# Last row blocks in float32 column groups, with w2's load and split moved, in a mixture-of-experts kernel on one core

## What is computed

```python
# x: (8, 256, 256) float32; x_rot = quaternion rotation of x times a spectral gate
logits = jnp.einsum('bsd,de->bse', x_rot, router_w) + router_b
top1 = jnp.argmax(softmax(logits), axis=-1)          # 8 experts
for i in range(8):
    h = jnp.einsum('bsd,df->bsf', x_rot, w1[i]) + b1[i]      # 256 -> 2 * 1024
    a, g = jnp.split(h, 2, axis=-1)
    y = jnp.einsum('bsh,hd->bsd', a * sigmoid(g), w2[i]) + b2[i]
    out = out + jnp.where((top1 == i)[..., None], y, 0.0)
return x + out
```

## Time and profile before

| | us |
|---|---|
| median of three runs | 216.72 |
| lowest, highest | 215.16, 495.23 |
| profiled execution | 216.05 |
| its span | 214.3 |
| granted TensorE clock, mean | 0.988 |

### The profile page before, as it was taken

How to read it: one execution, slowest core, us unless ns; L and a number is a source line. 1 busy time by engine, 2 the same in 40 slices (tenths; PEclk the granted TensorE clock), 3 DMA queues, 4 the chain that set the end, 5 groups by cost and what they waited for, 6 DMA issues and landing times.

```text
span 214.3 us, 4364 instructions
## 1 busy us (share of the span) xinstructions
PE 202.4 (94%) x1511; PEld 189.9 (89%) x1512; DVE 158.0 (74%) x308; ACT 122.2 (57%) x206; POOL 128.8 (60%) x163
## 2 busy tenths in 40 slices
PE   7999658999999999999999999999999999999992
PEld 3768524999999999999998999899999999999991
DVE  4839980589836997498889869994898469874960
ACT  2535841484918574567684868473939185745620
POOL 6004287775601878378778878887487818720752
PEclk9999997999999999999999999999999999999998
DMA  5994734979865174947499459827845691720011
GB/s 149 387 363 181 259 118 98 294 233 321 261 183 231 49 256 89 330 144 260 79 333 291 145 176 334 258 79 213 326 119 179 185 322 56 253 46 0 25 40 37
DMA packets 17540, 41.26 MB, mean 193 GB/s; under 512 B 2920, under 2 KB 11241, under 8 KB 15338
## 3 DMA queue, kind: packets, MB, share of 16 engines
q1 hardware_dynamic: 12784, 30.48, 40.0%
q0 software_dynamic: 4512, 10.50, 19.2%
q10 hardware_dynamic: 218, 0.01, 0.1%
HBM read 36.78 MB, written 6.03 MB: 200 GB/s over the span
## 4 chain that ended last, share of the span: by engine, by line
PE 65%; DVE 15%; issue 7%; POOL 6%; DMA 4%; ACT 3%; DVEq 0%; ACTq 0%
PE y_ps L1116 8%; PE y_ps L1117 8%; PE y_ps L1118 8%; PE g_ps L1096 6%; PE g_ps L1101 6%; PE g_ps L1097 5%; PE a_ps L1101 5%; PE a_ps L1097 5%; PE a_ps L1096 5%; DMA xg<-x_rows,g_idx 4%; PE y_ps L928 3%; DVE arena L821 3%; POOL out_dram L438 2%; POOL y_out L429 2%; DVE u_lo L827 2%
## 5 line engine op out<-in xcount | busy, mean ns | idle before, releaser
L438 POOL DMA_INDIRECT out_dram<-y_out,s_idx x30 | 44.0, 1465 | 42.5 <-DVE y_out L850 31.7
L573 ACT ACTIVATE arena<-g_ps,b_t 128x384 f32<-128x384 f32 (+1 forms) x64 | 34.5, 538 | 47.1 <-PE g_ps L1101 47.0
L821 DVE SCALAR_TENSOR_TENSOR arena<-a_ps,b_t,arena 128x384 f32<-128x384 f32 (+1 forms) x64 | 36.1, 563 | 31.2 <-PE a_ps L1101 28.4
L1116 PE MATMUL y_ps<-w_hi,u_hi 128*128 128x256 f32 x168 | 48.5, 289 | 0.1
L1117 PE MATMUL y_ps<-w_lo,u_hi 128*128 128x256 f32 x168 | 47.5, 283 | 0.0
L1118 PE MATMUL y_ps<-w_hi,u_lo 128*128 128x256 f32 x168 | 47.5, 283 | 0.0
L429 POOL DMA_INDIRECT y_out<-in_x_dram,g_idx x32 | 40.9, 1279 | 9.8 <-issue 9.8
L417 POOL DMA_INDIRECT xg<-x_rows,g_idx x32 | 36.5, 1141 | 14.9 <-issue 9.1
L579 ACT ACTIVATE u_hi<-arena 128x384 fp32r<-128x384 f32 (+1 forms) x64 | 30.7, 479 | 15.5 <-DVE arena L821 15.4
L712 DVE TENSOR_TENSOR w_lo<-w_raw,w_hi 128x1024 fp32r<-128x1024 f32 x32 | 37.2, 1221 | 1.8 <-ACT w_hi L526 1.4
L1096 PE MATMUL g_ps<-xr_hi,w_hi 128*128 128x256 f32 (+3 forms) x128 | 37.0, 302 | 0.6 <-ACT xr_hi L561 0.6
(11 more groups left out here) (167 smaller groups left out, 295.6 us busy)
## 6 DMA issues: line engine op xcount, KB each, us to landing
w_raw<-in_L_ffn_w_dram SPq DMA_DIRECT2D x16, 1024.0 KB, 8.2
w_raw<-in_L_ffn_w_dram SPq DMA_DIRECT2D x16, 512.0 KB, 5.0
arena<-in_x_dram SPq DMA_DIRECT2D x4, 512.0 KB, 5.9
x_rows<-arena SPq DMA_DIRECT2D x8, 256.0 KB, 3.0
b_all<-in_L_ffn_b_dram SPq DMA_DIRECT2D x1, 1024.0 KB, 5.1
xg<-x_rows,g_idx POOLq DMA_INDIRECT x32, 6.4
y_out<-in_x_dram,g_idx POOLq DMA_INDIRECT x32, 4.4
out_dram<-y_out,s_idx POOLq DMA_INDIRECT x30, 3.7
```

What stands on the lines that cost most here:

```text
L438: nc.gpsimd.indirect_dma_start(out=out_flat, out_offset=bass.IndirectOffsetOnAxis(ap=s_idx[:, i * NSUB + s:i * NSUB + s + 1], axis=0), in_ ...
L821: V.scalar_tensor_tensor(u32[:, c % (8 - SIG_RING), 0:n], pair[c % RING][0][:, 0:n], b1_t[:, bass.ds(e * (2 * NC) + c, 1)], sig[:, c % SIG ...
L1116: T.matmul(dst, u_hi[:, uv], w2_hi[:, wv], start=first, stop=False)
```

## The change

1. The size classes become 192, 256, 288, 320, 352, 512 (384 goes, 192 comes; class 192 uses the same first product as 256). Where the last block holds up to 32 or 64 tokens (classes 288, 320, 192), it is not computed from the split operands but by `part_block`: eight float32 matmuls, one per chunk, with 32 or 64 stationary columns of u32 and 256 moving columns of w2_raw. They go in turn to 4 or 2 groups of the array's columns, each group sums its own chunks in its own partitions of y_ps[1], and DVE adds the groups (`add_parts`: three adds of 32 rows or one of 64, each waiting for the one before).
2. u32 is kept whole (8 chunks, in the space of x_t) and w2_raw is kept until the second product ends. SP's load of w2 waits for mm2_done, and w1's load of the item after it comes behind w2's.
3. w2_hi_part goes from behind chunk 2 to behind chunk 4 on ACT, w2_lo_part from behind chunk 4 to behind chunk 5 on DVE.
4. Block 0 is computed ahead of blocks 2 and 1, and the part block stands in the place of the last one. The last item's adds and scatters follow this order.
5. ACT and DVE have five bodies per item (256, 288, 320, 384, 512 columns) for three.

```diff
-    SIZES = (256, 288, 320, 352, 384, 512)
+    SIZES = (192, 256, 288, 320, 352, 512)
+    PARTS = {size: (size // P, size % P) for size in SIZES if size % P in (32, 64)}
...
-            def load_tile(i, e):
+            def load_w1_again(i, e):
                 for u in range(W1U):
                     sp.wait_ge(w1_split[u], i)
                 for k in range(KH):
                     load_w1(e, k)
+            def load_w2_again(i, e):
+                sp.wait_ge(w2_split, i)
+                sp.wait_ge(mm2_done, i)
                 for h in range(W2U):
-                    sp.wait_ge(w2_split, i)
                     load_w2(e, h)
...
+            load_w1_again(1, 1)
             for e in range(1, NE):
-                load_tile(e, e)
+                load_w2_again(e, e)
+                if e + 1 < NE:
+                    load_w1_again(e + 1, e + 1)
...
+            def add_parts(i, word, sizes_here):
+                def of_sizes(left):
+                    if not left:
+                        dve.sem_inc(dve_chain, more)
+                        return
+                    s, wide = PARTS[left[0]]
+                    with dve.If(f_size(word) == SIZES.index(left[0])):
+                        rows = y_out[i % YB][0:wide, s * DIM:(s + 1) * DIM]
+                        for g in range(1, P // wide):
+                            link(V.tensor_tensor(rows, y_ps[1][g * wide:(g + 1) * wide, PLACE[s] * DIM:(PLACE[s] + 1) * DIM],
+                                                 rows, ALU.add))
...
+                    with dve.Else():
+                        count[0] = start
+                        of_sizes(left[1:])
...
+            def part_block(size, at1, at2, done=None):
+                s, wide = PARTS[size]
+                groups = P // wide
+                for c in range(NC):
+                    pe.wait_ge(pair_free[c], at2 if c >= CARRIED else at1)
+                    g = c % groups
+                    last = T.matmul(y_ps[1][g * wide:(g + 1) * wide, PLACE[s] * DIM:(PLACE[s] + 1) * DIM],
+                                    u32[:, c, s * P:s * P + wide], w2_raw[:, c * DIM:(c + 1) * DIM],
+                                    start=c < groups, stop=c >= NC - groups)
...
-                with pe.If(f_size(word) >= BLOCKS.index(3)):
+                row_blocks((0,), at1, done=outer_done)
+                with pe.If(f_size(word) >= SIZES.index(352)):
                     row_blocks((2,), at1)
-                row_blocks((1,), at1, done=outer_done)
-                row_blocks((0,), at1, done=mm2_done)
+                with pe.Else():
+                    with pe.If(f_size(word) == SIZES.index(320)):
+                        part_block(320, at1, at2)
+                    with pe.If(f_size(word) == SIZES.index(288)):
+                        part_block(288, at1, at2)
+                with pe.If(f_size(word) == SIZES.index(192)):
+                    part_block(192, at1, at2, done=mm2_done)
+                with pe.Else():
+                    row_blocks((1,), at1, done=mm2_done)
```

More of the change, by code:

```diff
@@ L49, in adaln_moe_ffn_kernel @@
     YB = 3
-    LANDINGS = (0, 1, 2, 3, 5)
+    LANDINGS = (1, 2, 3, 4)
     CONSTS = 9
@@ L280, in if_blocks, with if_width, word_registers @@
                     body(4)
+        def if_width(eng, word, body, low=0):
+            widths = (2 * P, 288, 320, 3 * P, ITEM)
+            firsts = (0, SIZES.index(288), SIZES.index(320), SIZES.index(352), SIZES.index(ITEM))
+            if low == len(widths) - 1:
+                body(widths[low])
+                return
+            with eng.If(f_size(word) < firsts[low + 1]):
+                body(widths[low])
+            with eng.Else():
+                if_width(eng, word, body, low + 1)
+        def word_registers(eng):
+            return [eng.alloc_register(f"word_at{a}") for a in range(2)]
         def word_register(eng, name):
@@ L846, in add_rows @@
+            def add_rows(i, word):
                 dve.wait_ge(mm2_done, i + 1)
                 dve.wait_ge(b2_added, i + 1)
-                for h in range(2):
-                    half = bank_rows(i, h)
-                    V.tensor_tensor(half, y_ps[h][:, :].rearrange("p (s d) -> p s d", s=2), half, ALU.add)\
-                        .then_inc(y_done[h], 1)
-            def add_last(i, blocks):
+                half = bank_rows(i, 0)
+                V.tensor_tensor(half, y_ps[0][:, :].rearrange("p (s d) -> p s d", s=2), half, ALU.add)\
+                    .then_inc(y_done[0], 1)
+                half = bank_rows(i, 1)
+                link(V.tensor_tensor(half, y_ps[1][:, :].rearrange("p (s d) -> p s d", s=2), half, ALU.add))
+                if word is not None:
+                    add_parts(i, word, list(PARTS))
+                dve.sem_inc(y_done[1], 1)
@@ L855, in add_last @@
+            def add_last(i, blocks, n, word):
                 dve.wait_ge(b2_added, i + 1)
                 dve.wait_ge(outer_done, i + 1)
-                rows = bank_rows(i, 1)[:, 0:min(blocks - 1, 2)]
-                V.tensor_tensor(rows, y_ps[1][:, :].rearrange("p (s d) -> p s d", s=2)[:, 0:min(blocks - 1, 2)], rows,
-                                ALU.add).then_inc(last_added, 1)
-                dve.wait_ge(mm2_done, i + 1)
                 for a in range(2 if blocks == NSUB else 1):
@@ L863, in add_last @@
                     V.tensor_tensor(rows, y_ps[0][:, a * DIM:(a + 1) * DIM], rows, ALU.add).then_inc(last_added, 1)
+                dve.wait_ge(mm2_done, i + 1)
+                rows = bank_rows(i, 1)[:, 0:min(blocks - 1, 2)]
+                link(V.tensor_tensor(rows, y_ps[1][:, :].rearrange("p (s d) -> p s d", s=2)[:, 0:min(blocks - 1, 2)], rows,
+                                     ALU.add))
+                add_parts(i, word, [size for size in PARTS if max(size, 2 * P) == n])
+                dve.sem_inc(last_added, 1)
                 dve.wait_ge(last_added, 3 if blocks == NSUB else 2)
```

77 lines of the change are left out of this document (48 added, 29 removed).

## The result

The changed kernel takes **238.19 us** (median of four runs, 236.15 to 241.6) where the kernel before took 215.94 on the same chip (median of four, lowest 214.4): ratio 1.1035, 95% interval 1.0972 to 1.1097. The run of 241.6 us and one of the kernel before, 495.23 us, fell in a slower state of the chip and are not in the ratio. I had forecast 218.2 with a range up to 221.5. The change makes the kernel slower by 22 us, and nothing in my range covers it.

What follows compares the result with a forecast made beforehand. PE, at 94% of the span, was taken as the bound; savings of PE work and added waits, summed by item, came to +2.0 us, giving 218.2 us, own range 216.0 to 220.6, stated range 213.0 to 221.5.

Steps and rivals of the forecast that it cites:

- The groups: PE's part blocks: about 1.0 us with groups of 32, 1.85 with 64, against 2.88 for a row block.
- The drain of the array: Rival on PE: each change of tiling mode drains the array, 1.6 us in all, 219.8 us; chance 0.05.
- The chain to w2's split: DVE and ACT work from the adds to w2_lo's end, making PE wait 0 to 1.65 us ahead of second products.
- extras: Work added behind DVE's adds: 0.43 us for three compares and a waited-for add, plus the groups' adds at 0.46 each.
- 6.07 for the chain: From gated(3) on DVE until w2 is split, with 256 columns: 6.07 us.
- The last u_lo: DVE's last u_lo before PE's second product comes later: 1.0 us more in items 1 and 6.
- a sign of being wrong: Item 4's gather on POOL: PE no longer waiting for it would show the forecast wrong; no size given.
- Bounds 0.1 and 0.9: Range in us for the three compares and waited-for add behind DVE's adds, put at 0.43.
- my rivals: Saving arrives, 211.0 us (0.20); w2 late, 221 to 224 (0.12); array drains, 219.8 (0.05); serial groups, 221 to 222 (0.03).
- w1's load at nothing: On SP, w1's load behind w2's is hidden by the first product, 11.5 us long at least, so costs nothing.
- w2 lands late: Rival: w2's DMA landing delays w2_hi and the second product in seven items, +3 to +5 us, 221 to 224; chance 0.12.
- The end of the kernel: Behind the last bank's add, DVE's part add, two compares and two linked waits: 0.8 us, all on the path.

Runs made afterwards that it cites:

- b_w2_late_2: Kernel before with only w2's load behind the second product and its split moved later: ratio 1.041; same edit as b_w2_late on another chip: 1.0183.
- after_kept_busy: Changed kernel plus one unused float32 matmul of 128 x 512 ahead of PE's wait for w2's split in each item: ratio 1.1052 to the kernel before.
- a_no_part_adds: Changed kernel without the compares and groups' adds on DVE in items 0 to 6: ratio 1.0168 to the kernel before.
- b_w2_split_moved: Kernel before with only w2's split moved later on ACT and DVE, the loads left where they were: ratio 1.0155.

## Why the prediction was wrong

**The groups (right).** 1.07 us for 1.0 and 1.95 for 1.85, both with the last matmul's tail. The drain of the array is hardly to be seen: a part block starts 0.20 to 0.32 us behind the start of the matmul before it, at full clock, where 0.12 is the pace. That is at most 0.2 us more, and PE's compares stand in the same place, so it may be either.

**The chain to w2's split (right in kind, too small).** The waits ahead of the second products, by item 1 to 7:

| | 1 | 2 | 3 | 4 | 5 | 6 | 7 | sum |
|---|---|---|---|---|---|---|---|---|
| forecast | 0 | 0.85 | 0.5 | 0.2 | 1.65 | 0.95 | 1.5 | 5.65 |
| measured | 0.88 | 1.50 | 1.44 | 1.17 | 1.47 | 1.49 | 2.32 | 10.27 |

The terms that were too small are "extras" of 0.43 (1.02 measured in item 7, 2.22 - 1.20), 6.07 for the chain (6.22 there, 6.34 in b_w2_late_2) and the hand-over from DVE to PE, which stood nowhere (0.30 there). A reader who measures a chain must measure to the waiting engine's start, not to the end of the last operation.

**The last u_lo (right).** The second products of items 1 and 6 take 9.51 us instead of 8.71, 0.80 more where I had 1.0.

**By item.** From one first product's start to the next, in us (item 7 to the end of the last matmul; "end" is from there to the end of the span):

| | 0 | 1 | 2 | 3 | 4 | 5 | 6 | 7 | end |
|---|---|---|---|---|---|---|---|---|---|
| before | 23.79 | 24.60 | 18.19 | 18.81 | 22.81 | 22.74 | 24.52 | 17.50 | 4.1 |
| changed | 23.78 | 26.44 | 23.36 | 21.22 | 22.41 | 26.30 | 27.06 | 20.38 | 7.3 |

I had forecast +0.5 for items 2 and 3 together, and they lose 7.6; for item 5 I had -0.3, and it loses 3.6. Item 0 gains nothing, though its part block saves 0.9 us: small pauses ahead of its last two chunks, its part block and item 1 take that back. And no turn waits for a gather any more, which I had named as a sign of being wrong: items 2 and 3 are late by DVE's chain now, and not by POOL.

**"Bounds 0.1 and 0.9" for the compares, and no term for the five bodies (the step that failed).** I took an item change's 0.24 us on ACT as the price of a branch and compare. That row is of a change with no packet of the instruction queue in its idle time. The five bodies are item 5 of the change, and the sum has no term for them; nor has it one for the compares' bodies that are stored and not run. Measured, the changes to items 1, 3, 4, 5 and 6 have idle time of 2.1 to 5.5 us on ACT or DVE. Five versions alone cost 8.6 us in the kernel before; the compares, run and stored, 8.2 in the changed one. None of my rivals was this.

**"w1's load at nothing".** The load did hide. w1's split did not, because DVE came to it late: 0.45 + 1.74 us.

**The turns.** Gate 5 frees the banks that the turns need. With w2_hi ahead of gate 5, the turn waits in items 2 and 5 (1.82, 0.63). I had looked only at what the second product waits for.

**The clock.** Not in the sum: about 5 us in the trace. In after_kept_busy, where a stretch moves to item 6, nothing of it is gained.

**w2 lands late (a rival).** It happened once:

```profile
96.36 1.92 ACT L562 ACTIVATE w_hi<-w_raw 128x2048 fp32r<-128x2048 f32 x1 [1.25 <-DMA w_raw<-in_L_ffn_w_dram]
```

in item 2, where w2 landed 9.2 us behind its issue; the median is 4.9. There it is not nothing: from gate 3 to the end of w2_lo it takes 7.57 us (94.18 to 101.75) for item 7's 6.22, and item 2 loses most. The same wait, 1.2 to 2.5 us, stands in item 2 in every trace of the changed kernel's variants with one buffer but a_no_part_adds, which has it in item 4 (2.2 us). In the kernel before, b_w2_late against b_w2_split_moved shows the late load to be worth 0.3%, less than the intervals.

**The end of the kernel.** Forecast 0.8; 3.2 measured. DVE's part is 0.9 (the last scatter starts 1.6 us behind the last matmul instead of 0.7). The other 2.3 us are behind that scatter: 5.6 us to the end of the span instead of 3.3. They are in every trace with five versions (5.6 to 5.9 us behind the scatter) but a_no_part_adds (3.6), and in none with three.

**The sum.** Against 215.4 us: w2 late alone 8.8, five versions alone 8.6, the compares 8.2, groups -6.3 of PE's work. They do not add: five versions are worth 8.6 on the kernel before and 3.2 on the changed one, and w2's late load and split 8.8 on the kernel before, but 16 on the changed one with three versions. That each lateness uses the slack that hid another is my explanation; no run separates it.

## What to carry to other kernels

A version of a loop body that is never taken can cost time (8.6 of 215 us here, 0.3% on another chip): count the code that an engine must jump past at each branch, and look whether the instruction queue has packets in its idle time. Before an edit is costed by its own instructions, ask which buffer it keeps alive longer. Here keeping w2 unsplit moved 4 us of work on two engines to the last moment, and a second buffer gives most of it back. And when several engines have under 1 us of slack each, small delays are not to be forecast one by one: a wait can bring a lower clock, and a late split brings a late turn.
